# A mamba block scan on one core: a decay computed after the turned copy, and two projections side by side

## The reference

```python
def step(h, inp):                       # over t, for every channel d (1024) and state n (16)
    u_t, d_t, b_t, c_t = inp
    dA = jnp.exp(d_t[..., None] * A)
    dBu = (d_t * u_t)[..., None] * b_t[:, None, :]
    h = dA * h + dBu
    y = jnp.einsum('bdn,bn->bd', h, c_t)
    return (h, y)
y = scan(step) + u * D_skip
y = y * jax.nn.silu(z)
out = y @ out_proj_w.T                  # 1024 -> 512
x = x + out                             # then the second layer on group-normalised x
```

## Time and profile before

| | |
|---|---|
| median of 3 runs | 4982.57 us (4982.34 to 4989.84) |
| the profiled execution | 4989.84 us, its span 4988.1 us |
| PE busy | 4655.8 us, 93% of the span |
| DVE busy | 4106.8 us, 82% |
| POOL busy | 3419.2 us, 69% |
| ACT busy | 2984.3 us, 60% |
| first scan, last gate of `scan` | 1227.02 us, 3834.10 us |
| scans on DVE (L1158) | x2048, 2431.4 us busy |
| POOL's products (L920) | x1024, 2397.7 us busy |
| granted PE clock, mean | 0.974 |

### The profile page before, as it was taken

The page is one execution under the profiler, slowest core; times in us unless marked ns, Lnnn a source line. Parts: engine busy times, 40 slices in busy tenths (PEclk is TensorE's granted clock), DMA queues, the critical chain, the costliest instruction groups (busy, mean ns, idle before and its releaser), DMA issues. The chain is left out here.

```text
span 4988.1 us, 120130 instructions
## 1 busy us (share of the span) xinstructions
PE 4655.8 (93%) x47160; PEld 2950.1 (59%) x47160; DVE 4106.8 (82%) x4324; ACT 2984.3 (60%) x6070; POOL 3419.2 (69%) x1712
## 2 busy tenths in 40 slices
PE   4999999993899999999999999999999699999999
PEld 4666666661455555555555555555554588887787
DVE  7888888872999999999999999999997667776332
ACT  2666666664777776767777777777764444554111
POOL 0576777765999999999999999999997222222000
PEclk9999999996999999999999999999999899999999
DMA  5344433433233323332333323332331111112453
GB/s 202 115 152 150 151 142 130 150 141 126 68 97 96 95 82 93 97 93 86 90 100 101 90 83 95 95 95 89 95 96 53 66 76 76 76 76 81 183 200 135
DMA packets 191783, 538.35 MB, mean 108 GB/s; under 512 B 15824, under 2 KB 15840, under 8 KB 181840
## 3 DMA queue, kind: packets, MB, share of 16 engines
q1 hardware_dynamic: 185920, 480.31, 28.8%
q0 software_dynamic: 5104, 51.35, 2.6%
q10 hardware_dynamic: 288, 0.00, 0.0%
HBM read 329.22 MB, written 202.38 MB: 107 GB/s over the span
## 5 line engine op out<-in xcount | busy, mean ns | idle before, releaser
L920 POOL TENSOR_TENSOR sc_hc<-sc_hc,sc_c_rep 128x1024 f32<-128x1024 f32 x1024 | 2397.7, 2369 | 170.0 <-ACT sc_state L941 167.7
L1158 DVE TENSOR_TENSOR_SCAN sc_hc<-sc_da,sc_state,sc_ring 128x512 f32<-128x512 f32 x2048 | 2431.4, 1260 | 51.1 <-PE sc_ring L1065 42.8
L980 ACT ACTIVATE sc_da<-sc_delta,l_neg_a 128x512 f32<-128x512 f32 x2048 | 1351.7, 707 | 0.0
L1065 PEld LDWEIGHTS sc_ring<-sc_diag,sc_dut 64*64 64x64 f32 x32768 | 890.1, 133 | 718.7 <-issue 718.6
L1065 PE MATMUL sc_ring<-sc_diag,sc_dut 64*64 64x128 f32 x32768 | 1102.3, 275 | 24.6 <-DMA sc_w_out<-in_w_out 17.2
L1075 PE MATMUL sc_y_ps<-sc_hc,sc_fold 128*64 128x512 f32 x4096 | 1004.7, 612 | 28.2 <-POOL sc_hc L920 21.7
L941 ACT ACTIVATE sc_state<-sc_hc 128x2 f32<-128x2 f32 x1024 | 206.0, 201 | 647.4 <-DVE sc_hc L1158 647.4
L1085 PE MATMUL sc_o_ps<-sc_yg,sc_w_out 128*128 128x512 f32 x1024 | 556.1, 630 | 2.9 <-ACT sc_o_sb L964 2.1
L1366 POOL TENSOR_TENSOR l_count<-l_count,as_oh 128x1024 f32<-128x1024 f32 x64 | 182.4, 2850 | 505.8 <-DVE as_oh L1549 505.8
L1075 PEld LDWEIGHTS sc_y_ps<-sc_hc,sc_fold 128*64 128x64 f32 x4096 | 251.1, 137 | 415.4 <-issue 379.6
L71 PE MATMUL fr_mm<-fr_xn_hi,l0f_w_in_hi 128*128 128x512 f32 x1024 | 438.4, 428 | 26.3 <-DVE fr_delta L671 11.8
(11 more groups left out here) (166 smaller groups left out, 6572.1 us busy)
## 6 DMA issues: line engine op xcount, KB each, us to landing
sc_duz<-spill SPq DMA_DIRECT2D x128, 768.0 KB, 5.9
sc_delta<-spill SPq DMA_DIRECT2D x256, 256.0 KB, 4.0
spill<-fr_z SPq DMA_DIRECT2D x64, 512.0 KB, 2.8
spill<-fr_u SPq DMA_DIRECT2D x32, 1024.0 KB, 8.7
spill<-fr_du SPq DMA_DIRECT2D x32, 1024.0 KB, 4.3
spill<-fr_delta SPq DMA_DIRECT2D x32, 1024.0 KB, 6.4
sc_c_rep<-bc SPq DMA_DIRECT2D x128, 256.0 KB, 4.4
soft<-as_et SPq DMA_DIRECT2D x16, 2048.0 KB, 6.3
```

Of the source, the lines that this page charges most:

```text
L920: nc.gpsimd.tensor_tensor(hc[:, p], hc[:, p], c_rep[:, 2 * q:2 * q + 2, :], ALU.mult).then_inc(s_hp, 1)
L980: nc.scalar.activation(da[:, p % 4, r, :], delta[:, i % 2, p % 2, :], ACT.Exp, scale=keep.neg_a[:, c:c + 1]).then_inc(s_da, 1)
L1065: done = nc.tensor.matmul(to[:, :, k::4], dut[rows, i % 2, k, HALF * h:HALF * h + HALF], diag[rows, u, 4 * q + c:4 * q + 4:2, k, :], start ...
L1158: nc.vector.tensor_tensor_scan(hc[:, p, r, :], da[:, p % 4, r, :], ring[:, SLOT[at], r::2], state[:, i, 2 * p + r:2 * p + r + 1], ALU.mult ...
```

## The change

Two places in `scan` are written in another order, and a table goes.

- ACT: in the body, `decays(g, i, p)` moves from ahead of the `if p == 5` part to behind it. For p other than 5 nothing moves. The waits of the copy, the skip and the column now stand ahead of the decays of pair 5.
- ACT: the table DIAGS = (2, 1, 2, 1, 1, 0, 1, 1) of how many diags are made at each p becomes 1 + (p == 0): 2, 1, 1, 1, 1, 1, 1, 1. Nine a block either way; one moves from p = 2 to p = 5.
- PE: the fourth step of a block's projection moves from behind `fill(*nxt, 0)` to ahead of it, next to the third.

```diff
@@ scan
-    DIAGS = (2, 1, 2, 1, 1, 0, 1, 1)
@@ scalar, body
                             keep_state(g - 1, KD - 1, p + PAIRS - AHEAD)
-                        decays(g, i, p)
                         if p == 5:
                             if i == 0 and more:
                                 keep_column(g + 1)
...
                             write_skip(g, i, i + 1 < KD or more)
+                        decays(g, i, p)
...
-                            for e in range(made, NDIAG if (i, p) == (KD - 1, PAIRS - 1) else made + DIAGS[p]):
+                            for e in range(made, NDIAG if (i, p) == (KD - 1, PAIRS - 1) else made + 1 + (p == 0)):
@@ tensor, body
                     if past:
-                        project(g - 1, 1 - u, i // 2, half + 2, half + 3)
+                        project(g - 1, 1 - u, i // 2, half + 2, half + 4)
                     if follows:
                         fill(*nxt, 0)
-                    if past:
-                        project(g - 1, 1 - u, i // 2, half + 3, half + 4)
-                    if follows:
                         fill(*nxt, 1)
```

## The result

The changed kernel takes 5069.96 us (median; 5059.48 to 5075.10) against 4983.36 for the kernel before: a ratio of 1.0163, interval 1.0148 to 1.0177. That is 87 us slower by the medians (81 by the ratio). Forecast were 5093 us, and 111 us slower. The profiled execution took 5062.96 us (span 5061.3), 73 us more than that of before. The stage from the first scan to the last gate went from 2607.1 us (1227.02 to 3834.10) to 2684.8 us (1219.87 to 3904.62), +77.7; what lies ahead of it was 7 us shorter and what follows 3 us longer, in code that the change doesn't touch.

What follows compares the result with a forecast made beforehand. Four nearly level engines, bound by a ring through ACT's state of pair 3, POOL, PE and the gate. Fourteen chunks 110.6, last chunk +6, first -6: +111 us on the 4982.57 median, 5093 us; own range 5073 to 5120, wider 5040 to 5135.

Steps and rivals of the forecast that it cites:

- one ring: Scan stage: scans, ACT's state of pair 3, POOL's pairs, PE's add_up 3, next gate; about 0.2 us slack in even blocks.
- ACT's order: At p = 5 decays and a diag behind dut copy and skip make state(3) start 1.47 us later, at 6.15.
- Even blocks: Blocks where POOL also does add_x: add_up 3 later, next gate at 21.36 us, 1.28 more than 20.08.
- my 7.9: Loss in us per chunk with projects: 1.14 for i = 0, 3 x 1.28 for even, 4 x 0.73 for odd blocks.
- Odd blocks: Blocks with statistics on DVE: POOL's path alone gives 20.14 us; late fill 0 makes it 20.81, +0.73.
- PE's order: Fill 7 to add_up 2 falls from 5.21 to 4.85 us, 0.36 less a block, hidden by PE's waits.
- The first chunk: Blocks without projects, long because the skip is late; skip 1.23 us sooner ends two DVE waits: some -6 us.
- PE alone sets the pace: Rival: ACT's lateness is lost in slack and the change gains 30 to 40 us, about 4948; chance 0.10.
- a lower clock: Rival: PE's new waits before add_up 1 and add_up 3 lower its granted clock, 178 us, 5270; chance 0.06.
- the edits cancel: Rival: the two edits cancel, or ACT doesn't wait; within 10 us of 4983; chance 0.04.
- Ring A alone: Rival: only even blocks' path through POOL lengthens, fill 0 in time, odd blocks 20.14: +75 us, 5057; chance 0.22.
- the bound from above: Every odd block loses as much as an even one: 10.1 us a chunk, +147 us, 5130.

Runs made afterwards that it cites:

- experiment 5: Only the table DIAGS replaced, against the kernel before: 4978.52 us, ratio 1.0000.
- experiment 4: The changed kernel, but with the state of pair 3 kept between the skip and the decays of pair 5: 4944.68 us, ratio 0.9938 to the kernel before.
- experiment 1: Both ACT edits as in the changed kernel, PE's order as before: 5074.95 us, ratio 1.0199 to the kernel before.

## Why the prediction was right, and where it was off

- The bound. Four nearly level engines and one ring with 0.2 us of slack in even blocks: borne out by experiment 5, which lengthened the ring by 0.24 us and lost 0.04 to 0.13 of it.
- ACT's order: right in its mechanism, and shown by experiment 4: not the late decays cost, but the state of pair 3 behind them. The step of 1.47 us was met to the hundredth in odd blocks.
- Even blocks: the term that was mis-sized. Forecast 21.36, measured 20.87 in the block shown and 20.94 in the mean. I had put the turn at G plus a constant. It hangs on add_up 3, not on the gate, and behind a gate that DVE reaches late (2.46 us behind the add_up's start, not 1.99) the turn comes 0.47 us sooner after the gate, and with it the copy and state 3. My own sum had odd blocks end on DVE, and I didn't carry that on into the next block. Experiment 1 takes that lateness away and gets the 21.34 of the constant. Three such blocks a chunk are 1.3 us of my 7.9. A block i = 0 follows such a gate too: most take some 21.35, +0.4, not +1.1 (+0.55 in the mean). The last block of a chunk lost 0.3 us, not the 0.73 of an odd one. A chunk behind the first came out 5.6 us longer on the average ((3904.62 - 1382.08 - 3834.10 + 1395.82) / 15), not 7.8 (110.6 + 6, over 15).
- Odd blocks: forecast 20.81, measured 20.91. Fill 0 behind two projects is the end there, as said. But close below it lies an end that the prediction left out, PE's own work behind the late add_up 1: 20.80 with PE's order as before (experiment 1), some 20.44 with the new one (8.83 + 9.62 + 1.99). So a fill 0 in time would not have brought the odd blocks back to 20.14.
- The first chunk: -6 forecast; up to the gate that opens the second one it took 162.2 us in place of 168.8, -6.6. That is luck. The step "its blocks last long because the skip is late" was wrong: already the row of add_up 0 in the earlier trace rows puts its wait down to POOL, and in experiment 5 the first chunk takes 161.6 us with the skip as late as before. The long blocks stand where the granted clock was 0.50.
- PE's order: the saving of 0.36 us a block was right (5.21 to 4.86), its worth was not. I gave it nothing for itself; alone it is worth 16 us, in the changed kernel 12 (medians) to 18 (profiles), and 25 beside the kept state of experiment 4.
- The rivals: PE alone sets the pace, and a lower clock, fell in the changed profile (PE waits twice in even blocks and once in odd ones; PEclk 1.00). That the edits cancel fell by the result. "Ring A alone" named 5057, nearer to the measured 5070 than one would like, but for another reason: odd blocks did lose 0.83 us, and even ones less than it says.
- A slip in the sum: the bound from above, +147 us, leaves out the -6 of the first chunk; with it, it is some +142. Nothing hangs on it.
- Open: why the runs of one kernel scatter by 20 to 25 us within one experiment (the kernel before between 4962 and 4996 in all). Its runs with the higher mean clock are the shorter ones (4972.9 us in the mean at 0.977, 4985.5 at 0.974), but which stretches make the difference only a profile could tell.

## What to carry to other kernels

Ask of each instruction that also releases another engine what stands ahead of it in its queue, and what that waits for; an engine with over a quarter of the stage's time idle can set the pace by one late signal of 0.2 us. When engines are level, follow the ring for two rounds and not one: an event placed at a constant distance from a gate moves when another engine begins to end the gate. And undo an edit by parts: here one of the two was worth 16 us of gain, and keeping one state ahead of the decays made the whole 32 us faster than the kernel before.

## What the runs showed of the hardware

- A piece of matmuls that follows its own kind starts some 0.18 us sooner: taking two changes of array shape out shortened PE's stretch from 5.21 to 4.86 us. That much was in the rows; that over a third of it (16 of 43 us) reaches the run time beside a full DVE was not expected.
- The length of one wait doesn't tell whether PE's granted clock falls. Waits of 0.65 and 0.83 us in a block left it at 1.00. One of 1.56 us was followed by 0.50 in the first chunk of the kernel before, and left it at 1.00 in that of experiment 5. There the low clock was worth over a microsecond a block: 20.47 us against 19.35.
